# Inverse deviations by an integer guess and three Newton steps on VectorE, in a convolution, attention and experts block

## What is computed

```
def _ln_t(v, eps=1e-05):
    m = jnp.mean(v, axis=-1, keepdims=True)
    s = jnp.var(v, axis=-1, keepdims=True)
    return (v - m) / jnp.sqrt(s + eps)
...
t = t + _L1_attn_ref(_ln_t(t), w_qkv, w_out, b_out)
t = t + _L1_ffn_ref(_ln_t(t), Wr, W1, b1, W2, b2)
```

## Time and profile before

| what | value |
|---|---|
| time, median of 3 runs | 1309.75 us (1306.08 to 1310.2) |
| the profiled execution's own time | 1310.52 us |
| its span | 1308.7 us |
| TensorE busy | 1151.3 us (88%) |
| VectorE busy | 792.5 us (61%) |
| ScalarE busy | 630.8 us (48%) |
| GpSimd busy | 577.6 us (44%) |
| mean granted clock of TensorE | 0.936 |

### The profile page before, as it was taken

One profiled execution on the slowest core, in us unless ns is written; L12 is line 12 of the kernel. 1 busy time (PEld: TensorE's weight loads), 2 busy tenths in 40 slices (PEclk: granted clock), 3 DMA queues, 4 the chain that ended last, 5 costly groups with the idle time before them and its releaser, 6 DMA issues. The chain is left out here.

```text
span 1308.7 us, 29280 instructions
## 1 busy us (share of the span) xinstructions
PE 1151.3 (88%) x10343; PEld 759.2 (58%) x10343; DVE 792.5 (61%) x1425; ACT 630.8 (48%) x1129; POOL 577.6 (44%) x455
## 2 busy tenths in 40 slices
PE   3999799996589999999999998159999999999993
PEld 2555454644334444445445444049999999998772
DVE  2546545565578878778877871735565556555540
ACT  0636356464257756775776675223333333333332
POOL 1314224241358865276257526434444444444330
PEclk9989899896679999999999999569999999999996
DMA  4126652443412323232142413712333323332227
GB/s 125 50 65 208 272 168 88 139 144 110 129 41 55 79 77 73 73 97 90 43 110 78 106 43 100 269 34 41 49 50 49 51 49 50 49 50 43 41 32 263
DMA packets 99246, 120.47 MB, mean 92 GB/s; under 512 B 29400, under 2 KB 76440, under 8 KB 98488
## 3 DMA queue, kind: packets, MB, share of 16 engines
q1 hardware_dynamic: 78152, 70.29, 18.3%
q0 software_dynamic: 20544, 42.22, 14.5%
q10 hardware_dynamic: 432, 6.29, 1.2%
HBM read 72.97 MB, written 45.60 MB: 91 GB/s over the span
## 5 line engine op out<-in xcount | busy, mean ns | idle before, releaser
L823 ACT ACTIVATE WB<-PP 128x512 f32<-128x512 f32 x512 | 268.5, 606 | 167.5 <-PE PP L1132 167.4
L1449 DVE TENSOR_REDUCE mxp<-PP 128x2 f32<-128x1024 f32 x256 | 301.3, 1218 | 66.4 <-PE PP L1065 65.1
L868 ACT ACTIVATE WORK<-PP,b1c 128x256 f32<-128x256 f32 (+1 forms) x320 | 143.5, 449 | 258.4 <-PE PP L896 254.8
L633 POOL TENSOR_TENSOR WB<-WB 128x1024 f32<-128x1024 f32 x80 | 188.6, 2358 | 79.5 <-PE PP L1121 71.3
L896 PE MATMUL PP<-WORK,WB 128*128 128x256 f16 (+1 forms) x1920 | 207.9, 264 | 3.2 <-DVE WORK L1750 3.1
L1244 PE MATMUL PP<-WB,WORK 128*128 x1704 | 193.8, 273 | 0.0
L896 PEld LDWEIGHTS PP<-WORK,WB 128*128 x1920 | 176.6, 99 | 29.6 <-issue 4.2
L1244 PEld LDWEIGHTS PP<-WB,WORK 128*128 128x128 f16 x1704 | 164.4, 98 | 20.9 <-issue 0.4
L1132 PE MATMUL PP<-WORK 97*128 97x256 f16 x1024 | 160.6, 281 | 8.5 <-ACT WB L823 5.4
L601 POOL TENSOR_TENSOR WB<-WORK,WB 128x1024 f16<-128x1024 f32 x32 | 68.1, 2129 | 218.4 <-ACT WORK L734 218.4
L697 POOL DMA_INDIRECT res_d<-WORK,lb x71 | 115.7, 1630 | 102.8 <-DVE WORK L1777 87.5
(11 more groups left out here) (255 smaller groups left out, 1169.4 us busy)
## 6 DMA issues: line engine op xcount, KB each, us to landing
WORK<-in_L_ffn_W_dram POOLq DMA_DIRECT2D x32, 512.0 KB, 4.3
res_d<-WORK SPq DMA_DIRECT2D x8, 1024.0 KB, 4.5
late_d<-WB POOLq DMA_DIRECT2D x1, 6144.0 KB, 18.7
WB<-late_d ACTq DMA_DIRECT2D x3, 2048.0 KB, 17.8
WORK<-in_x_dram SPq DMA_DIRECT2D x8, 512.0 KB, 3.8
v_d<-WORK SPq DMA_DIRECT2D x4, 1024.0 KB, 4.8
WORK<-q_hi_d SPq DMA_DIRECT2D x16, 256.0 KB, 3.9
WORK<-v_d SPq DMA_DIRECT2D x8, 512.0 KB, 5.6
```

What stands on the lines that cost most here:

```text
L633: pool.tensor_tensor(PS[n % 2], PR[n % 3][:, 0], PR[n % 3][:, 1], ALU.add).then_inc(s("pair_kept"), 1)
L823: act.activation(PR[n % 3][:, c // 2, c % 2 * 2:c % 2 * 2 + 2], SCORES[m % 3] .rearrange("p (h n) -> p h n", h=2), ACT.Exp).then_inc(s("e_ ...
L868: act.activation(hid[u][:, k, 0:width], hidden_bank(k)[:, 0:width], ACT.Gelu, bias=b1c[:, bass.ds(e, 1), k], scale=1.0 / WSCALE)\
L1449: dve.tensor_reduce(mxp[:, n // 4 % 2, i, h:h + 2, k], PP[2 + h // 2][:, :].rearrange("p (h n) -> p h n", h=2), X_AXIS, ALU.max).then_inc( ...
```

## The change

In the three tails inside the attention, the mean and variance move from step 13 to step 12. ScalarE's square root of step 14 and VectorE's reciprocal of step 15 go. In their place VectorE computes the inverse root of the variance itself: half of the bits of the number, taken as an integer, subtracted from a constant, give a first guess, and three Newton steps y = y * (1.5 - 0.5 * v * y * y) refine it, one in each of the steps 13, 14 and 15. Two new constants and one small buffer come with it. In VectorE's step the new work stands behind the reductions and ahead of `tail_pick`. The fourth tail keeps the square root and the reciprocal.

```diff
-VAR_AT, SD_AT, RSTD_AT = 13, 14, 15
+VAR_AT, ROOT_AT, RSTD_AT = 12, (13, 14, 15), 15
+ROOT_BITS = 1597463007.0
...
+        root = sb("root", [P, 4, NT], F32)
...
-                    if t == SD_AT:
-                        tail_deviations(b)
...
+            def tail_roots(part):
+                bits, y, half, sq = root[:, 0], root[:, 1], root[:, 2], root[:, 3]
+                dve.drain()
+                if part == 0:
+                    dve.tensor_scalar(bits.bitcast(I32), small[:, 1].bitcast(I32), 1, None, ALU.logical_shift_right)
+                    dve.tensor_scalar(half, small[:, 1], -0.5, None, ALU.mult)
+                    dve.drain()
+                    dve.tensor_scalar(y.bitcast(I32), bits.bitcast(I32), -1.0, ROOT_BITS, ALU.mult, ALU.add)
+                    dve.drain()
+                dve.tensor_tensor(sq, y, y, ALU.mult)
+                dve.drain()
+                dve.tensor_tensor(sq, sq, half, ALU.mult)
+                dve.drain()
+                dve.scalar_tensor_tensor(out=small[:, 3] if part == 2 else y, in0=sq, scalar=1.5, in1=y,
+                                         op0=ALU.add, op1=ALU.mult)
+
             def tail_rstd(n):
-                dve.wait_ge(s("sd1_kept"), n)
+                dve.wait_ge(s("sd1_kept"), 1)
                 dve.reciprocal(small[:, 3], small[:, 2])
+                tail_shift(n)
+
+            def tail_shift(n):
                 dve.drain()
...
+                    if t in ROOT_AT:
+                        tail_roots(ROOT_AT.index(t))
                     if t == RSTD_AT:
-                        tail_rstd(b)
+                        tail_shift(b)
```

## The result

The changed kernel takes 1313.82 us in the median of 12 runs (1310.52 to 1318.18), the kernel before 1308.95 us (12 runs on the same chip, 1306.08 to 1310.88). The ratio is 1.0039 with a 95% interval of 1.0027 to 1.0052: some 5.1 us slower, between 3.5 and 6.8. The forecast was +3.0 us on the median known then, with 1312.8 us and a range that holds the result.

A forecast was written before the change was run, and what follows sets the result against it. VectorE was taken as a second bound beside ScalarE in the tails' steps, so added work counts and the removed stall is hidden: 2.1 + 0.6 + 0.5 - 0.2 = +3.0 us, giving 1312.8 us, range 1306.5 to 1317.0.

The forecast's parts named there:

- VectorE is a second bound: Steps 12 to 18: VectorE occupied for 20.6 of 21.3 us, with 0.74 us to spare in the undisturbed batch.
- The lateness of the reductions: VectorE, batch 2: moved statistics and added root instructions delay reductions by 1.1 us in step 13, up to 2.32, then 2.11.
- The spacing of 0.245 us: VectorE's new root instructions in steps 13 to 15: small dependent instructions follow each other by 0.245 us.
- step 16: VectorE in batch 2: nothing changes in steps 16 and 17, so the delay stays at 2.32 us.
- the 0.21 us of idle time ahead of step 18: VectorE's wait for a group in batch 2: used up by the delay, lowering it from 2.32 to 2.11 us.
- The stretches: Steps 14 to 19 of the three tails get longer by 2.1 us in batch 2, 0.6 and 0.5 in the others.
- about 21.6 us from step 14 to 19: Length of the stretch between these steps' first exponentials in all three batches, before 20.99, 19.47 and 21.04 us.
- The sum: Three tails: 2.1 + 0.6 + 0.5 = 3.2 us, less 0.2, so +3.0 us, passed on to the end in full.
- The 0.2 us taken off at the end: Step 18: TensorE also waited a little for ScalarE where it no longer will, so 0.2 us off the sum.
- A: Three tails: only ScalarE's stall matters, added work falls into VectorE's idle time, 9.8 us come back, 1300 us; chance 0.12.
- B: Three tails: a draw through closer spacing of small instructions and a clock that no longer dips, -1 to +1.5 us; chance 0.18.
- C: TensorE's clock dips more as it waits in steps 13 to 17, three times 1.5 us on top, 1317.3 us; chance 0.15.

The follow-up runs named there:

- the removal alone: Kernel before, with ScalarE's square root left out of the three tails and VectorE's reciprocal taking the variance, nothing moved: ratio 0.9968.
- the fastest kernel: Kernel before, with ScalarE's root, VectorE's reciprocal and its shift replaced in the three tails by guess, three Newton steps and shift on GpSimd: ratio 0.9953.

## Why the prediction was right

**That VectorE is a second bound**: shown, by the removal alone (0.9968, with the same 0.95 us wait) and by the price of each Newton step.

**The lateness of the reductions**, step by step in batch 2: forecast 1.1, 1.43, 2.17, 2.32, 2.32 and 2.11 us for the steps 13 to 18, measured 1.14, 1.46, 2.19, 2.25, 2.47 and 2.37. The spacing of 0.245 us was 0.24. Two terms are off. In step 16, where I had said that nothing changes, one picking instruction lasts 0.43 us (at 647.83) where it lasted 0.23, and that is the error of step 17; why is open. And the 0.21 us of idle time ahead of step 18 that I let the delay use up gave only 0.10 back, which makes the last term the worst, 0.26 short.

**The stretches**: +2.1, +0.6 and +0.5 forecast, +2.05, +0.78 and +0.45 measured from step 13 to 19. The "about 21.6 us from step 14 to 19" was misread by me: it is the new length counted from where step 14 used to begin. Step 14 itself begins 0.9 us late, as I had written two paragraphs earlier, so the stretch from its new start is 20.59 us in batch 2. In batch 1 VectorE sits idle for 0.54 us, put down to issue, ahead of the first root instruction (0.19 in the others); a gap of that kind stands there in the kernel before too (0.44), so it is not the change's.

**The sum**: 3.0 us forecast, 3.28 in the stretches, 5.1 (3.5 to 6.8) on the first chip and 3.6 (1.8 to 5.4) on the second. The forecast's total was thus too low on the first. The 0.2 us taken off at the end were not seen (3.2 without them). What it lacks besides is not in the steps it priced. It took the delay of these steps to be passed on with nothing added, and 1.2 us more lie between the tails. The stretch of batch 2 began 0.74 us later than the shift explains, and TensorE waits there for the load of values:

```profile
582.34 0.83 PE L1132 MATMUL PP<-WORK 97*128 97x256 f16 x6 [0.88 <-DMA WORK<-v_d]
```

SyncE's queue just ahead of it, in the changed kernel (first line the row of maxima, second the sums, third the values):

```profile
575.48 1.23 SPq L429 DMA_DIRECT2D WORK<-nmr  x2
576.75 1.31 SPq L447 DMA_DIRECT2D rcp<-WB  x1
578.11 0.48 SPq L372 DMA_DIRECT2D WORK<-v_d  x1
```

The second takes 1.31 us to issue here and 0.56 before. Whether this is caused by the change stays open. Against it: with no root at all the profile has three such waits too, 2.9 us, and the fastest kernel 3.4. The profile of the kernel before is from one chip only, so I have no fair count of it.

**The rivals.** A is refuted by the removal alone. B, a draw (-1 to +1.5 us), is excluded by the intervals, clearly on the first chip (from 3.5 us) and barely on the second (from 1.8). C, more dips, didn't happen: the granted clock was under 1 in one of the three stretches, two before. It was under 1 in all three with five steps and with the move undone, and there it hid, as VectorE waited for no group. Its counterpart is real on the other side: in the kernel before, the batches 1 and 3 with a dip are 1.5 and 1.7 us longer than batch 2. With no root and no dip they are still 0.44 and 0.17 us longer, so the dips themselves cost some 1.1 and 1.5 us. Both versions without the stall and without VectorE's extra work have none.

**The two rules.** The Trainium skill, in "VectorE: DVE Perf Modes", section "The TRN2 errata", gives (N+151)/0.96 ns for an fp32 addition, as an estimate 166 ns for eight elements. The profile agrees (0.17 us), but the price to reckon with was the spacing, 0.24. The Trainium skill, in "ScalarE: Activation LUTs", section "Table sets: the hidden batching unit", says that an exponential followed by a root costs about 5.3 us. In the trace the loads and the root took 2.81 us, and taking them away gave 4.2 us for three, since most was covered.

## What to carry to other kernels

Before moving work off an engine that visibly stalls the pipeline, add up the program of the engine that takes it over, step by step, in just those steps, with the time between instructions that depend on each other. VectorE is 61% busy over the span; in the 21.3 us of these steps it is 89% busy and waits for another engine in only 0.74 us. Taking a stall away is worth only what lies between it and the next bound (4.2 of 9.8 us), while each dependent instruction put on that next bound costs its start-to-start spacing, not its duration. Look for the engine that is idle in those very steps, even if it is slower: GpSimd needed 6.9 us for the root and made the kernel 6.2 us faster.

## What the runs showed that I had not expected

A delay of 0.93 us in the exponentials of step 14 was harmless where VectorE's added work set the pace (the changed kernel, with the move or without it), and cost its full length in the stretches, with the ratio pointing to more, where ScalarE's stall followed it (the move alone, 1.0042). And GpSimd's small instructions of 128x8 take 0.19 to 0.25 us and follow each other, drained, by 0.34 to 0.38 us, but between its second and third there were 1.48 us of idle time that the profile puts down to issue, in batch 2 (1.47 in batch 3, but 0.15 in batch 1).
